# Third stage of an eight-block kernel: two lanes nine rounds ahead of the other two, and the first and last steps of each attention beside other lanes' rounds

## The chip, the cores and the metric

The kernel runs on one core of a Trainium2 chip. The metric is the device time of one execution in microseconds (us). TensorE is called PE, VectorE DVE, ScalarE ACT, GpSimd POOL and SyncE SP.

## The reference, cut to what matters

The input is x, 4096 tokens of 128 channels (16 sequences of 256), and the program is eight blocks in a row, each `x = x + layernorm(block(layernorm(x)))`. The change touches the third of four stages, which holds three of the blocks: `L2_attn`, `L2_ffn` and `L3_attn`.

```python
x = x + ln(L2_attn(ln(x)))   # causal attention, 16 heads of 8 channels
x = x + ln(L2_ffn(ln(x)))    # gelu(x @ w1 + b1) @ w2 + b2, hidden 512
x = x + ln(L3_attn(ln(x)))   # a state space scan, an MLP, causal attention, an MLP

# inside L3_attn
n = rms_norm(xm); vg = n @ in_proj_w          # value and gate, 256 each
value = silu(conv4(value)); Bm, Cm = xm @ B_proj_w, xm @ C_proj_w
y = selective_scan(value, A, Bm, Cm, dt, chunk)
xm = xm + scale * (y * silu(gate) @ out_proj_w)
xm = xm + scale * mlp(rms_norm(xm))           # square(relu(n @ fc)) @ proj
q, k = rope(rms_norm(n @ q_w)), rope(rms_norm(n @ k_w))   # 16 query heads, 4 key heads
y = softmax(causal(q @ k.T)) @ v
xa = xa + scale * (y @ o_w); xa = xa + scale * mlp(rms_norm(xa))
```

## The kernel before

The 4096 tokens are eight groups of 512 tokens (two sequences of 256 each). In stage 3 they go through in two halves of four groups; the four groups of a half are the four *lanes* 0 to 3. A lane has a quarter of the buffer `LN`, a slice of `wAB` for scratch, and two of the eight PSUM banks: lane 0 banks 0 and 1, lane 1 banks 2 and 3, lane 2 banks 4 and 5, lane 3 banks 6 and 7.

Every engine has its own instruction stream, written out in a fixed order by Python generators: a lane's work on an engine is a generator, and each `yield` ends a *round*. `together(gens, lag)` takes one round of each lane in turn, and lane n begins n rounds after lane 0 (`LAG3` is 1). An instruction waits for the semaphores of the engines that it needs, and everything behind it on its engine waits with it.

Stage 3 (`phase3`) is five steps: `l2_in` (normalise, queries, keys, values of the L2 attention), `mid` (output product of that attention, the L2 MLP, the scan, an MLP, and queries, keys, values of the L3 attention), `l3_out` together with `l2_in` of the second half, `mid` again, and `l3_out`. Behind each of the first four steps comes an attention over all lanes (`attend`). In rounds of a lane, `l2_in` has 4, `l3_out` 6 and `mid` 53. Of the 53 rounds of `mid`, rounds 0 to 10 are the L2 output and MLP with five normalisations and the convolution (the *prelude*); rounds 11 to 42 are the scan, two times 16; rounds 43 to 52 (the *tail*) are the MLP (its second product in round 47, PE line L331, with DVE lines L1460 to L1456 and the statistics L237 behind it) and the rotated queries and keys (DVE lines L1554 to L1586 and L1488, in rounds 50 to 52).

An attention works on 32 *quads* (eight for each lane, in the order of the lanes), in 41 steps t from -5 to 35. In step t PE makes the scores of quad t by key in banks 4 to 7 (L388, L395), from which ACT takes the exponentials, and the scores of quad t+5 by query in banks 0 to 3 (L391, L398), from which DVE takes the maxima (L491), both with masks (L378). Each has a first and a second half. So steps -5 to -1 hold scores by query alone, and steps 28 to 35 scores by key, values (L475) and the transposes of results alone (L444, L465). The first exponential of the attention is in step 0.

At the end of stage 2 the four chunks of its result `YA` for each half are scaled, normalised and added to x (`dve_out`, `pool_out`), for all eight groups, before stage 3 begins; POOL gives the reciprocal root of each normalisation (L283).

SP issues nothing in stage 3 but one weight load at its start.

Of the kernel before, what the change touches and what calls it, by code (L numbers as in the profile page):

```python
# [18 lines left out]
LW = 8192  # L19
LAG2, LAG3 = 9, 1  # L20
# [118 lines left out]
def together(gens, lag=0, start=None):  # L139

    live, rnd = dict(enumerate(gens)), 0
    while live:
        for n in sorted(live):
            if rnd >= (start[n] if start else lag * n):
                try:
                    next(live[n])
                except StopIteration:
                    del live[n]
        rnd += 1
# [10 lines left out]
def build(nc, tables, wa, wb, wc, wd, wm, wi, ve, co, step, xin, out):  # L160
    ctx = ExitStack()
    with ctx:
# [197 lines left out]
        PT = [LN[:, LW * i + 6656:LW * i + 8192].rearrange("p (j c) -> p j c", j=4) for i in range(4)]  # L360
        OS = LN[:, 6144:6400].rearrange("p (t c) -> p t c", t=2)
        ON = [LN[:, LW * i + 6144:LW * i + 6400].rearrange("p (t c) -> p t c", t=2) for i in (1, 2)]
# [59 lines left out]
        def pe_attend(pe, banks, k, quads, nb, nw):  # L422
            n = len(quads)
            for t in range(-nb - 1, n + 4):
# [41 lines left out]
                if ins is not None:  # L466
                    ins.then_inc(*P4.inc((k, t, "second")))

        def pe_values(pe, quads, window):
            po = spare(6)  # L470
            for s in window:
                for kt, qt in ((0, 0), (0, 1), (1, 1)):
                    for j in range(4):
                        p = 128 * (kt + qt)
                        ins = pe.e.matmul(po[32 * j:32 * j + 32, qt, :], quads[s].v(kt, j), PT[s % 4][:, j, p:p + 128],  # L475
                                          start=s == window[0] and kt == 0, stop=s == window[-1] and kt == qt)
            return ins

        def dve_attend(dve, k, quads, nb, nw):
# [4 lines left out]
            for x in ON:  # L484
                ins = dve.e.memset(x, 0.0)
            ins.then_inc(*D4.inc())
# [6 lines left out]
            for t in range(-nb - 1, n + 4):  # L493
# [36 lines left out]
                D4.mark((k, t, "second"))  # L530

        def act_attend(act, k, quads, nb, nw):
            n = len(quads)
            for t in range(n + 4):
                w, on = window_at(t, nw, quads), done_at(t - 3, nb, nw, quads)
                if t < n:
                    act.wait_ge(P4, (k, t, "first"))
                    act.e.activation(PT[t % 4][:, 0:2, :], pair(4), ACT.Exp).then_inc(*A4.inc())  # L538
# [7 lines left out]
                if t < n:  # L546
                    act.wait_ge(P4, (k, t, "second"))
                    act.e.activation(PT[t % 4][:, 2:4, :], pair(6), ACT.Exp).then_inc(*A4.inc())  # L548
# [3 lines left out]
                A4.mark((k, t, "second"))  # L552

# [1161 lines left out]
        phi = wAB[:, 0:2048]  # L1715
        MR = MISC[:, 4:36].rearrange("p (m b) -> p m b", m=2)
# [266 lines left out]
        def dve_ya(dve, c, other, q, p):  # L1983
            k, m, gp = ("smoe", q), p // 2, p % 2
            al = views2(c, m)["al"]
            for n in range(2):
# [51 lines left out]
        def dve_out(dve, c, g):  # L2038
            dve.wait_ge(DD[LANES], "rls")
            YG = YA.rearrange("p b m e -> p (b m) e")[:, 4 * g:4 * g + 4, :]  # L2040
# [6 lines left out]
        def pool_out(pool, c, g):  # L2047
            yield from pool_norm(pool, c, (g, "so"))

# [278 lines left out]
        def phase3(eng, ls, l2_in, mid, l3_out, attend):  # L2328

            def stage(eng, c, item):  # L2330
                half, make = item
                yield from make(eng, c, 4 * half + c.n)

            for step, ka in (([(0, l2_in)], ("l2", 0)), ([(0, mid)], ("l3", 0)), ([(0, l3_out), (1, l2_in)], ("l2", 1)),
                             ([(1, mid)], ("l3", 1)), ([(1, l3_out)], None)):
                together([chain(stage, eng, c, step) for c in ls], LAG3)
                if ka is not None and attend is not None:
                    attend(ka, quads23(ls, ka), 4, 2)

        def pe_program(e):  # L2340
# [8 lines left out]
            def attend(ka, quads, nb, nw):  # L2349
                pe_attend(pe, banks, ka, quads, nb, nw)  # L2350
# [27 lines left out]
        def act_program(e):  # L2378
# [5 lines left out]
            def attend(ka, quads, nb, nw):  # L2384
                act_attend(act, ka, quads, nb, nw)
# [21 lines left out]
        def dve_program(e):  # L2407
# [9 lines left out]
            def attend(ka, quads, nb, nw):  # L2417
                dve_attend(dve, ka, quads, nb, nw)
# [13 lines left out]
            run_lanes(dve_out, dve, 1)  # L2432
# [13 lines left out]
        def pool_program(e):  # L2446
# [10 lines left out]
            run_lanes(pool_out, pool, 1)  # L2457
            ended(GD, "p2")
            sync_all(pool, "p2")
            phase3(pool, lanes(), pool_l2_in, pool_mid, pool_l3_out, None)  # L2460
# [206 lines left out]
```

## Time and profile before

| what | value |
| --- | --- |
| median of 3 runs | 3795.21 us (3792.87 to 3801.27) |
| the profiled execution | 3797.36 us |
| its span in the profile | 3795.6 us |
| busy share of the span | PE 78%, DVE 63%, ACT 48%, POOL 14% |
| granted PE clock, mean | 0.868 of full |
| DMA, mean | 7 GB/s |

Busy time is the time in which an engine ran instructions; the rest of the span it waited. The granted clock has two levels, 0.5 (1.2 GHz) and 1.0 (2.4 GHz), and a stretch shows the mean of both. Stage 3 lies between 2031.5 and 3476.7 us of the span. In the trace's windows and timelines the start of a row is in us from the span's start.

### The profile page before, as it was taken

To read this page: it belongs to the slowest core of one execution; us is meant where nothing else is said; L and a number is where in the kernel's file an instruction comes from. 1 tells how busy PE (TensorE), PEld (TensorE's weight loads), DVE (VectorE), ACT (ScalarE), POOL (GpSimd) and SP (SyncE) were. 2 spreads that over 40 slices of the span, in tenths; PEclk is the share of its full clock that TensorE was granted. 3 is DMA by queue.
4 is the path that set the end of the run, shared out by engine and by line. 5 is a ranking of instruction groups with operands and counts; after the bars stand their busy time and mean duration, and the time that the engine had idled before them with its cause. 6 is when DMAs were issued, how large, how long until landed. Compare 5 with 4: busy or idle time off the path is not lost.

```text
span 3795.6 us, 76097 instructions
## 1 busy us (share of the span) xinstructions
PE 2975.8 (78%) x31950; PEld 2354.3 (62%) x31950; DVE 2390.8 (63%) x6446; ACT 1816.6 (48%) x3876; POOL 516.4 (14%) x643
## 2 busy tenths in 40 slices
PE   6788887778888758778884887967778798686885
PEld 3466665456666547667774765856666486574564
DVE  4655555565554578888897666467565845755337
ACT  3556555555555467777773443324434332343222
POOL 1110001120100132222222011120010202002000
PEclk7889988888998879898997988987989899697887
DMA  2000000000000010000000000000000000001000
GB/s 86 1 1 1 1 1 1 1 1 1 1 1 1 1 51 6 7 9 6 7 1 12 2 2 1 2 1 2 2 1 3 1 2 1 1 3 45 1 1 23
DMA packets 13542, 27.99 MB, mean 7 GB/s; under 512 B 784, under 2 KB 9232, under 8 KB 12688
## 3 DMA queue, kind: packets, MB, share of 16 engines
q1 hardware_dynamic: 13200, 23.12, 1.8%
q8 instruction: 252, 4.13, 0.5%
q14 instruction: 90, 0.74, 0.1%
HBM read 21.02 MB, written 2.10 MB: 6 GB/s over the span
## 4 chain that ended last, share of the span: by engine, by line
PE 50%; DVE 36%; ACT 10%; issue 3%; POOL 1%; DMA 0%; SPq 0%; DVEq 0%; POOLq 0%; ACTq 0%
PE ps L331 6%; DVE LN L1944 5%; PE ps L322 4%; PE ps L1822 3%; PE ps L1303 3%; DVE RS L237 3%; PE ps L388 3%; PE ps L296 3%; PE ps L475 3%; DVE M L491 2%; DVE LN L1957 2%; ACT LN L268 2%; PE ps L1314 2%; DVE LN L258 2%; PE ps L1766 1%
## 5 line engine op out<-in xcount | busy, mean ns | idle before, releaser
L304 ACT COPY LN<-ps 128x512 f32<-128x512 f32 (+4 forms) x592 | 303.3, 546 | 629.4 <-PE ps L296 172.2
L283 POOL TENSOR_TENSOR RS<-RS,MISC 128x4 f32<-128x4 f32 x216 | 219.2, 1015 | 2177.2 <-DVE RS L249 1642.6
L296 PE MATMUL ps<-cons,LN 128*128 128x128 f32 x672 | 143.2, 356 | 349.7 <-DVE LN L256 124.8
L296 PEld LDWEIGHTS ps<-cons,LN 128*128 128x128 f32 x672 | 97.8, 178 | 403.7 <-DVE LN L256 143.9
L491 DVE TENSOR_REDUCE M<-ps 128x6 f32<-128x768 f32 x256 | 242.0, 955 | 140.1 <-PE ps L475 95.7
L1944 DVE TENSOR_TENSOR LN<-LN 128x1024 f32<-128x1024 f32 (+2 forms) x192 | 220.3, 1147 | 27.8 <-ACT LN L304 16.9
L388 PE MATMUL ps<-LN 32*128 32x256 f32 x1024 | 187.4, 440 | 53.3 <-DVE LN L527 32.1
L632 DVE TENSOR_REDUCE M<-ps 128x12 f32<-128x1536 f32 x64 | 112.4, 1756 | 175.2 <-PE ps L378 175.2
L322 PE MATMUL ps<-LN,wAB 128*128 128x512 f32 x384 | 207.1, 672 | 14.3 <-ACT LN L341 8.5
L1822 PE MATMUL ps<-LN,wAB 128*128 128x128 f32 x1024 | 150.9, 310 | 74.3 <-ACT LN L304 73.8
L391 PE MATMUL ps<-LN 32*128 32x256 f32 x1024 | 202.9, 475 | 0.8 <-DVE M L491 0.8
L331 PE MATMUL ps<-wAB,LN 128*128 128x128 f32 x1536 | 197.9, 291 | 4.8 <-DVE LN L1469 4.0
L331 PEld LDWEIGHTS ps<-wAB,LN 128*128 128x128 f32 x1536 | 193.0, 207 | 13.1 <-DVE LN L1469 6.3
L1868 ACT ACTIVATE LN<-LN,RS 128x128 f32<-128x128 f32 x512 | 198.7, 400 | 1.6 <-DVE RS L1969 0.6
L2026 POOL TENSOR_TENSOR LN<-LN,M 128x2048 f32<-128x2048 f32 x32 | 146.3, 4571 | 357.2 <-DVE M L1976 357.2
L1822 PEld LDWEIGHTS ps<-LN,wAB 128*128 128x128 f32 x1024 | 143.6, 224 | 78.2 <-ACT LN L304 77.3
L548 ACT ACTIVATE LN<-ps 128x768 f32<-128x768 f32 x128 | 103.7, 810 | 172.0 <-PE ps L475 135.3
L1995 DVE SCALAR_TENSOR_TENSOR LN<-LN,RS,ps 128x128 f32<-128x128 f32 x480 | 127.7, 340 | 48.3 <-PE ps L1822 48.3
L538 ACT ACTIVATE LN<-ps 128x768 f32<-128x768 f32 x128 | 103.8, 811 | 108.6 <-PE ps L378 88.5
L237 DVE BATCH_NORM_STATS2 RS<-LN 128x6 f32<-128x128 f32 x608 | 132.5, 281 | 30.2 <-ACT LN L304 26.0
L1766 PE MATMUL ps<-wAB,LN 128*128 128x128 f32 x1024 | 126.6, 282 | 24.3 <-ACT LN L304 22.9
L388 PEld LDWEIGHTS ps<-LN 32*128 32x128 f32 x1024 | 83.0, 191 | 90.3 <-issue 40.1
(345 smaller groups left out, 7563.3 us busy)
## 6 DMA issues: line engine op xcount, KB each, us to landing
wAB<-wb SPq DMA_DIRECT2D x16, 256.0 KB, 2.7
LN<-wd SPq DMA_DIRECT2D x8, 512.0 KB, 6.9
wAB<-wa SPq DMA_DIRECT2D x1, 3840.0 KB, 16.1
wCs<-wc SPq DMA_DIRECT2D x1, 2336.0 KB, 10.7
XA<-xin SPq DMA_DIRECT2D x8, 256.0 KB, 7.6
y<-XA SPq DMA_DIRECT2D x8, 256.0 KB, 2.3
wAB<-wb SPq DMA_DIRECT2D x1, 1024.0 KB, 5.0
wAB<-wm SPq DMA_DIRECT2D x1, 1024.0 KB, 4.8
```

Source lines behind the costliest of these rows:

```text
L237: dve.e.bn_stats(r[:, 6 * i:6 * i + 6], src[:, i, :]).then_inc(*c.D.inc((k, "stats", i)))
L283: pool.e.tensor_tensor(c.r[:, 40:44], c.r[:, 36:40], mhalf, ALU.pow).then_inc(*c.G.inc((k, "rstd")))
L296: ins = pe.e.transpose(ps[:, n * 128:(n + 1) * 128], src[:, n, :], ident)
L304: act.e.copy(dst, ps).then_inc(*c.A.inc(named(k, done)))
L322: pe.e.matmul(ps[:, :], w1[:, j * 128:(j + 1) * 128], xT, start=True, stop=True).then_inc(*c.P.inc((k, "up", j)))
L331: ins = pe.e.matmul(ps[:, t * 128:(t + 1) * 128], h3[:, j, t * 128:(t + 1) * 128], w2[:, j, :], start=j == 0, stop=j == nh - 1)
L388: pe.e.matmul(psum[n][:, 0:256], qt.ka[rows[j], o:o + 128], qt.qa[rows[j], o:o + 256], start=True, stop=False)
L391: pe.e.matmul(psum[n][:, 128:384], qs.qa[rows[j], o + 128:o + 256], qs.ka[rows[j], o:o + 256], start=True, stop=False)
L491: return dve.e.tensor_reduce(cols[:, 2 - 2 * h:4 - 2 * h, :, q.at], src, X_AX, ALU.max, negate=True)
L1822: ins = pe.e.matmul(psum[2 * gp + n][:, i * 128:(i + 1) * 128], eTb[2 * gp + n][:, i * 128:(i + 1) * 128], v["ym"][:, 4 * g + i, :], start ...
L1868: ins = act.e.activation(v["L3"][:, b, :], v["L3"][:, b, :], ACT.Exp, bias=v["nm"][:, b:b + 1], accum_out=v["rs"][:, b:b + 1])
L1944: dve.e.tensor_tensor(dst, src[:, 0:n, :], src[:, n:2 * n, :], op).then_inc(*c.D.inc())
```

## The change

`phase3` now runs lanes 0 and 1 (*front*) and lanes 2 and 3 (*back*) as two pairs, each with a lag of 1 inside. In each step but the first the back pair starts 9 rounds behind the front pair (`SKEW3`; 2 in the first, which is where it stood). The attention's generators yield after each step, on every engine. Its steps -5 to -1 stand behind the rounds of the back pair, once the front pair has ended its rounds; its steps 0 to 27 stand alone, as before; and its last eight steps, 28 to 35, stand ahead of the first eight rounds of the next step of stage 3. The next step of stage 3 still begins only when the steps 0 to 27 have been put down.

The buffers that the attention used in all lanes' parts of `LN` (exponentials `PT`, results `OS` and `ON`) move to parts of lanes 2 and 3 and of `wAB` that nothing else uses then; there are three buffers of exponentials, in two halves each, where there were four. Two memsets of `ON` go. Of the end of stage 2, `dve_out` and `pool_out` are done for four groups there; for the other four they stand in the first attention, on DVE in its steps 5 to 12, half of a group in each step. For that the last accumulation of stage 2 writes to `wAB` (`YF`) in place of `YA`.

```diff
+def abreast(gens, lag):
+    live, rnd = dict(enumerate(gens)), 0
+    while live:
+        for n in sorted(live):
+            if rnd >= lag * n:
...
+        if live:
+            yield True
+        rnd += 1
...
-        PT = [LN[:, LW * i + 6656:LW * i + 8192].rearrange("p (j c) -> p j c", j=4) for i in range(4)]
...
+        HALVES = [LN[:, LW * c + o:LW * c + o + 768] for c in (2, 3) for o in (6144, 6912)]
+        HALVES += [wAB[:, 1024 * c:1024 * c + 768] for c in (0, 1)]
+        PT = [[x.rearrange("p (j c) -> p j c", j=2) for x in HALVES[2 * i:2 * i + 2]] for i in range(3)]
...
-        def dve_attend(dve, k, quads, nb, nw):
+        def dve_attend(dve, k, quads, nb, nw, side):
...
                 D4.mark((k, t, "second"))
+                if t >= 5:
+                    next(side, None)
+                yield
...
+                        dst = YF if q == 15 else YA
...
+        def dve_out_later(dve, ls):
+            for c in ls:
+                yield from dve_out(dve, c, c.n + 4)
+                yield
...
-                together([chain(stage, eng, c, step) for c in ls], LAG3)
-                if ka is not None and attend is not None:
-                    attend(ka, quads23(ls, ka), 4, 2)
+            ending, skew = iter(()), 2
...
+                front = abreast([stage(c, items) for c in ls[:2]], LAG3)
+                back = abreast([stage(c, items) for c in ls[2:]], LAG3)
+                coming = attend(ka, quads23(ls, ka), 4, 2) if ka else iter(())
+                rnd, ramp, more, last = 0, 5, True, True
+                while last:
+                    next(ending, None)
+                    more = more and next(front, False)
+                    if rnd >= skew:
+                        last = next(back, False)
+                    if not more and ramp and last:
+                        next(coming, None)
+                        ramp -= 1
+                    rnd += 1
+                for _ in ending:
+                    pass
+                for _ in range(ramp + 32 - 5 + 1):
+                    next(coming, None)
+                ending, skew = coming, SKEW3
...
-            run_lanes(dve_out, dve, 1)
+            together([dve_out(dve, c, c.n) for c in lanes()], 1)
```

Line numbers in the changed kernel are higher: for PE, L388 and L395 are now L405 and L412, L391 and L398 are L408 and L415, L378 is L395, L475 is L493, L296 is L311, L314 is L329, L322 is L337, L331 is L346, L1303, L1314, L1324, L1330 are L1322, L1333, L1343, L1349.

On PE, where an attention ends and `mid` begins, there stood before the last scores, the last values (L475) and transposes, and then the output products of two lanes (L314), the transposes (L296) and the first MLP products (L322):

```order
L388 MATMUL ps<-LN 128x256 x2
L395 MATMUL ps<-LN 128x128 x2
L378 MATMUL ps<-cons 128x2x32 x8
L465 MATMUL ps<-cons,LN 128x128 x2
L475 MATMUL ps<-LN 32x128 x24
L465 MATMUL ps<-cons,LN 128x128 x2
L444 MATMUL ps<-cons,LN 128x128 x2
L314 MATMUL ps<-wCs,LN 128x128 x8
L296 MATMUL ps<-cons,LN 128x128 x4
```

Now the output products of lanes 0 and 1 (L329) stand between the scores of the steps 28 to 31:

```order
L329 MATMUL ps<-wCs,LN 128x128 x4
L405 MATMUL ps<-LN 128x256 x2
L412 MATMUL ps<-LN 128x128 x2
L395 MATMUL ps<-cons 128x2x32 x8
L405 MATMUL ps<-LN 128x256 x2
L412 MATMUL ps<-LN 128x128 x2
L395 MATMUL ps<-cons 128x2x32 x8
L482 MATMUL ps<-cons,LN 128x128 x2
L329 MATMUL ps<-wCs,LN 128x128 x4
```

What moved there is eight steps of the attention, which now stand ahead of one round of the front pair each.

On PE, at the end of `mid`, there stood before the tail of four lanes, in which every second product of the MLP (L331) has the transposes of the lane ahead of it (L296) in front:

```order
L331 MATMUL ps<-wAB,LN 128x128 x16
L322 MATMUL ps<-LN,wAB 128x512 x4
L1255 MATMUL ps<-wCs,LN 128x192 x4
L296 MATMUL ps<-cons,LN 128x128 x4
L331 MATMUL ps<-wAB,LN 128x128 x16
L322 MATMUL ps<-LN,wAB 128x512 x2
L1255 MATMUL ps<-wCs,LN 128x192 x4
L296 MATMUL ps<-cons,LN 128x128 x4
```

Now the front pair's tail has scan products of the back pair in it (L1333, L1356, L1343, L1349):

```order
L346 MATMUL ps<-wAB,LN 128x128 x16
L337 MATMUL ps<-LN,wAB 128x512 x2
L1343 MATMUL ps<-wAB,LN 32x128 x8
L1349 MATMUL ps<-cons,LN 128x128 x4
L1333 MATMUL ps<-LN 128x128 x8
L311 MATMUL ps<-cons,LN 128x128 x4
L346 MATMUL ps<-wAB,LN 128x128 x16
L1356 MATMUL ps<-LN 128x32 x4
```

and the back pair's tail has the attention's steps -5 to -1 in it, here two halves of one step (L408, L415, L395) ahead of the second MLP product:

```order
L408 MATMUL ps<-LN 128x256 x2
L415 MATMUL ps<-LN 128x128 x2
L395 MATMUL ps<-cons 128x2x32 x8
L408 MATMUL ps<-LN 128x256 x2
L415 MATMUL ps<-LN 128x128 x2
L395 MATMUL ps<-cons 128x2x32 x8
L346 MATMUL ps<-wAB,LN 128x128 x16
L337 MATMUL ps<-LN,wAB 128x512 x2
```

What moved is that a tail of four lanes is now two tails of two lanes, the first beside scans and the second beside the attention's start.

On DVE, in the first attention, two maxima of a step (now L506) and the division of a window (L539, L542) are followed by the work of `dve_out` on a group of the second half (L2064 scaling, L252 to L264 statistics, L273 and L305 the sum into x), which before stood at the end of stage 2:

```order
L539 RECIPROCAL MISC<-ps 128x16
L542 TENSOR_TENSOR LN<-ps,MISC 128x8x8 x2
L2064 TENSOR_SCALAR wAB<-wAB,MISC 128x128 x4
L252 BN_STATS RS<-wAB 128x6 x4
L255 BN_AGGR RS<-RS 128x2 x4
L264 TENSOR_SCALAR RS<-RS 128x4
L506 TENSOR_REDUCE M<-ps 128x2x3 x2
L532 TENSOR_TENSOR M<-M 128x16
L273 TENSOR_SCALAR wAB<-wAB,RS 128x128 x4
L305 TENSOR_TENSOR XA<-XA,wAB 128x512
```

What moved there is half of a group's work behind each of eight steps.

## Rows read from the trace of the kernel before

**Rows 1.** The page's part 1: busy time of each engine, share of the span, instructions.

```profile
PE 2975.8 (78%) x31950; PEld 2354.3 (62%) x31950; DVE 2390.8 (63%) x6446; ACT 1816.6 (48%) x3876; POOL 516.4 (14%) x643
```

**Rows 2.** Windows of stage 3: stretch, length, busy per engine, PEclk, DMA.

```profile
2031.50:2073.60 42.10, 0.07 (x1) 0.02 (x1) 37.54 (x171) 0.00 (x0) 11.14 (x11) 0.56 0.07 25
...
2073.60:2114.00 40.40, 34.06 (x262) 23.85 (x266) 23.28 (x63) 15.52 (x25) 8.89 (x9) 0.71 0.00 1
...
2114.00:2214.80 100.80, 87.38 (x2422) 75.08 (x2423) 64.88 (x114) 50.05 (x76) 0.00 (x0) 0.98 0.01 3
...
2214.80:2602.80 388.00, 307.40 (x2688) 243.14 (x2692) 239.55 (x717) 124.67 (x222) 59.34 (x72) 0.85 0.00 1
...
2702.80:2819.80 117.00, 87.07 (x736) 65.25 (x740) 71.56 (x228) 35.31 (x57) 20.04 (x20) 0.83 0.00 1
...
2919.30:3299.10 379.80, 298.45 (x2688) 237.36 (x2692) 239.48 (x717) 124.71 (x222) 59.37 (x72) 0.87 0.00 1
...
3399.30:3476.70 77.40, 53.29 (x474) 40.46 (x474) 43.86 (x153) 19.78 (x33) 8.05 (x8) 0.89 0.00 1
```

**Rows 3.** Windows inside the first middle, 2214.8 to 2602.8, same columns.

```profile
2214.80:2235.70 20.90, 18.45 (x266) 14.54 (x267) 1.84 (x9) 7.51 (x12) 0.00 (x0) 0.67 0.01 2
2235.70:2282.50 46.80, 34.63 (x187) 24.08 (x185) 40.12 (x191) 18.28 (x28) 15.16 (x15) 0.88 0.00 1
2282.50:2321.00 38.50, 21.46 (x77) 13.72 (x78) 33.63 (x113) 11.98 (x20) 9.26 (x9) 0.77 0.00 1
2321.00:2475.00 154.00, 154.00 (x1652) 127.68 (x1651) 76.40 (x174) 52.65 (x91) 16.53 (x28) 0.98 0.01 2
2475.00:2586.00 111.00, 62.19 (x322) 49.30 (x320) 76.98 (x217) 31.28 (x67) 18.39 (x20) 0.75 0.00 0
2586.00:2602.80 16.80, 16.67 (x196) 13.82 (x196) 10.58 (x15) 2.97 (x5) 0.00 (x0) 0.50 0.01 1
```

**Rows 4.** Timeline of PE, tail of the middle: start, us, line, idle before.

```profile
2495.85 3.74 PE L331 MATMUL ps<-wAB,LN 128*128 128x128 f32 x32
...
2509.87 5.72 PE L331 MATMUL ps<-wAB,LN 128*128 128x128 f32 x32
...
2524.10 1.02 PE L296 MATMUL ps<-cons,LN 128*128 128x128 f32 x4 [3.78 <-DVE LN L256]
...
2524.91 5.05 PE L331 MATMUL ps<-wAB,LN 128*128 128x128 f32 x32
...
2538.92 1.12 PE L296 MATMUL ps<-cons,LN 128*128 128x128 f32 x4 [5.93 <-DVE LN L256]
```

**Rows 5.** Timeline of DVE, the same tail.

```profile
2515.62 0.69 DVE L1460 TENSOR_TENSOR LN<-ps,vecs 128x512 f32<-128x512 f32 x1 [6.79 <-PE ps L331]
...
2520.59 2.48 DVE L1469 SCALAR_TENSOR_TENSOR LN<-ps,LN 128x512 f32<-128x512 f32 x4
...
2522.98 1.06 DVE L256 TENSOR_SCALAR LN<-LN,RS 128x128 f32<-128x128 f32 x4
...
2574.74 0.82 DVE L1554 TENSOR_TENSOR wAB<-LN 128x640 f32<-128x640 f32 x1
...
2576.45 0.20 DVE L1558 TENSOR_SCALAR wAB<-wAB 128x80 f32<-128x80 f32 x1
...
2577.88 0.64 DVE L1561 RECIPROCAL wAB<-wAB 128x80 f32<-128x80 f32 x1
...
2582.20 0.63 DVE L1586 COPY LN<-LN 128x128 f32<-128x128 f32 x4
...
2584.05 1.41 DVE L1488 TENSOR_SCALAR LN<-ps,cons 128x512 f32<-128x512 f32 x2 [1.21 <-PE ps L296]
```

**Rows 6.** Groups of DVE in the first steps of the second attention.

```profile
L491 DVE TENSOR_REDUCE M<-ps 128x6 f32<-128x768 f32 x10 | 9.6, 958 | 4.2 <-PE ps L378 4.2
```

**Rows 7.** Timelines of PE and DVE, lane 0 in the last item.

```profile
3414.73 1.06 PE L314 MATMUL ps<-wCs,LN 128*128 128x128 f32 x8
...
3451.69 0.69 DVE L290 TENSOR_TENSOR XA<-XA,LN 128x512 f32<-128x512 f32 x1
```

More of the change, by code:

```diff
@@ L530, in dve_attend @@
                 D4.mark((k, t, "second"))
+                if t >= 5:
+                    next(side, None)
+                yield
         def act_attend(act, k, quads, nb, nw):
             n = len(quads)
-            for t in range(n + 4):
+            for t in range(-nb - 1, n + 4):
                 w, on = window_at(t, nw, quads), done_at(t - 3, nb, nw, quads)
-                if t < n:
+                if 0 <= t < n:
                     act.wait_ge(P4, (k, t, "first"))
-                    act.e.activation(PT[t % 4][:, 0:2, :], pair(4), ACT.Exp).then_inc(*A4.inc())
+                    act.e.activation(PT[t % 3][0], pair(4), ACT.Exp).then_inc(*A4.inc())
                 if on is not None:
@@ L545, in act_attend @@
                 A4.mark((k, t, "first"))
[L546 removed]
+                if 0 <= t < n:
                     act.wait_ge(P4, (k, t, "second"))
[L548 removed]
+                    act.e.activation(PT[t % 3][1], pair(6), ACT.Exp).then_inc(*A4.inc())
                 if w is not None:
@@ L2328, in phase3, with stage @@
         def phase3(eng, ls, l2_in, mid, l3_out, attend):
[L2330 to L2335, printed above, removed]
-                together([chain(stage, eng, c, step) for c in ls], LAG3)
-                if ka is not None and attend is not None:
-                    attend(ka, quads23(ls, ka), 4, 2)
+            def stage(c, items):
+                for half, make in items:
+                    yield from make(eng, c, 4 * half + c.n)
+            ending, skew = iter(()), 2
+            for items, ka in (([(0, l2_in)], ("l2", 0)), ([(0, mid)], ("l3", 0)), ([(0, l3_out), (1, l2_in)], ("l2", 1)),
+                              ([(1, mid)], ("l3", 1)), ([(1, l3_out)], None)):
+                front = abreast([stage(c, items) for c in ls[:2]], LAG3)
[16 more added lines that the diff above has]
+                ending, skew = coming, SKEW3
         def pe_program(e):
@@ L2456, in pool_program, with attend @@
                 pool_half(pool, chains(), h)
-            run_lanes(pool_out, pool, 1)
+            together([pool_out(pool, c, c.n) for c in lanes()], 1)
             ended(GD, "p2")
             sync_all(pool, "p2")
-            phase3(pool, lanes(), pool_l2_in, pool_mid, pool_l3_out, None)
+            def attend(ka, quads, nb, nw):
+                yield from idle(10)
+                if ka == ("l2", 0):
+                    for c in lanes():
+                        for _ in pool_out(pool, c, c.n + 4):
+                            pass
+                yield from idle(len(quads) + 4 - 5)
+            phase3(pool, lanes(), pool_l2_in, pool_mid, pool_l3_out, attend)
             ended(GD, "p3")
```

28 lines of the change are left out of this document (16 added, 12 removed).

## The prediction

> **What bounds the kernel now.** I read the page first: PE is busy 78% of the span and DVE 63% [rows 1], so neither is full, and a mean over stages says little. Then I cut stage 3 into windows at the first exponential of attention step 0 and of step 28 [rows 2]. The reader is to see three kinds of stretch. Where the attention is alone (steps 0 to 27) 100.8 us hold 87.4 us of PE at clock 0.98: nearly full. The two long stretches between a step 28 and the next step 0 (I call each a *middle*) take 388.0 and 379.8 us. The short ones are 40.4, 117.0 and 77.4 us, and ahead of them lie 42.1 us in which DVE is busy 37.5 and PE not at all.
>
> The windows inside a middle [rows 3] show that its limits change. The scan is PE alone: 154.0 of 154.0 us busy, DVE half idle at 76.4. The prelude and the tail are neither: in the tail's 111.0 us PE is busy 62.2 and DVE 77.0, at clock 0.75. The timelines say why [rows 4, 5]. The transposes of one lane and of the next (2524.10, 2538.92) start 14.8 us apart, and between them the engines take turns: PE's L331 5.1 to 5.7 us, DVE's scaling, mixing and statistics 5.0 (2515.62 to 2520.59), L1469 of two other lanes 2.5, L256 1.1, and PE transposes again. Four lanes one round apart all need the same engine at once. The attention's ends [rows 3] are thin too: 20.9 us for its last eight steps, with 1.8 us of DVE, and 16.8 us for its first five, with 10.6 us of DVE, at clock 0.67 and 0.50.
>
> **The change, part by part.** The sum is made against the profiled execution, 3797.4 us, 2.2 above the median.
>
> *End of stage 2.* Eight groups take 42.1 us and 37.5 us of DVE, 4.7 a group [rows 2]. Four stay, so 19 us go. The other four cost 18.8 us of DVE inside an attention in which DVE has 64.9 busy in 100.8 us. In the eight steps that take them DVE has 8 x (64.9/28 + 2.35) = 37.3 us to do, where a step lasts 3.6 us, 28.8 in all. The cover is thus 8.5 us too short; DVE can lag some microseconds behind PE with banks in hand, so I take 6 (ends 0 and 8.5). In the first step of the stage the lanes stand as before, but about two of the five first attention steps and the memsets are hidden: 4 us. Together -17.
>
> *The middle.* Rounds 0 to 52 of the front pair and rounds 9 to 62 of the back pair; five parts.
> 1. Rounds 0 to 8, front alone with attention steps 28 to 35. Four lanes need 46.8 us until lane 0's second transposes [rows 3]. For two lanes PE and DVE in strict turns would be (34.6 + 40.1)/2 = 37.4, with ACT and POOL between them; I take 42. The eight attention steps hold 18.5 us of PE work and wait only on PE and ACT; most falls into PE's waits, I add 7. **49** (ends 42 and 54).
> 2. Rounds 9 to 20, front in convolution and scan, back in the prelude. DVE: half a prelude (40.1 + 33.6)/2 = 36.9, the front's own convolution rounds 11, twelve rounds of a pair's scan at 76.4/32/2 = 1.2, 14: 62. Three rounds in between, in which the back pair is in its MLP, are PE's and leave DVE idle some 5 us each: **76** (ends 65 and 84).
> 3. Rounds 21 to 42, all in the scan: 22 x 154.0/32 = **106**. Nothing is gained there.
> 4. Rounds 43 to 53, front in the tail, back in the scan. Turns as now: rounds 43 to 46 some 5.1 each, 20.5 (statistics or L256, transposes, ACT, halves of the MLP, 1.2 of scan; my estimate), then L331 3.7 (at full clock) [rows 4], then DVE 5.0, L1469 1.4, scan of two lanes 1.2, L256 0.9, transposes 0.7, L331 3.7: 12.9; then 5.0 + 1.2 + 0.9; then the rope rounds, of which the last statements take 4.9 and 1.4 [rows 5] and the first 1.9 (2574.74 to 2576.65): 1.9 + 1.2, 4.9 + 1.9 + 1.2, 1.4 + 4.9 + 1.2, 1.4. That makes 64; I take **65** (ends 58 and 77). PE's scan lies inside DVE's turns.
> 5. Rounds 54 to 62, back alone with attention steps -5 to -1. The same turns without the scan, 50; each of the five steps adds two maxima of 0.96 us [rows 6] and, where PE's 3.3 us for it (16.7/5 [rows 3]) are not covered, some more: 10; half clock on two products of L331 (5.7 against 3.7) 4. **64** (ends 50 and 75).
>
> Sum 360, against 388.0 and 379.8: **-28 and -20**. All ends together give 321 and 396.
>
> *The stretch of 117.0 us* (`l3_out` and the second `l2_in`, ten rounds). With a skew of nine the pairs follow each other. Half of PE's and DVE's work in turns would be about (87.1 - 18 - 15 + 71.6 - 2 - 10)/2 = 57; two such are 114, and some overlap inside a pair and one round between the pairs make 45 + 55. Attention steps add 6: **106, -11** (ends 90 and 125).
>
> *The last stretch, 77.4 us.* Lane 0 among four takes from 3414.7 to 3452.4, 37.7 us [rows 7]; a pair 34. Two in a row 68, minus the overlap, plus attention steps 5: **72, -5** (ends 65 and 82).
>
> Steps 0 to 27 of each attention keep their instructions and their order on every engine: 0. Three buffers in place of four cost nothing: the buffer that step t writes was read in step t-1 or earlier, which PE has passed.
>
> Sum: -17 - 28 - 20 - 11 - 5 = **-81**. 3797.4 - 81 = 3716, and on the scale of the median 3714.
>
> A weighing of the skill. Trainium skill, Perfetto Trace Analysis, Optimization Strategy, says that where the most contended engine changes from regime to regime, interleaving the regimes can help. The trace agrees that there are such regimes (154.0 us of PE alone beside 77.0 of 111.0 on DVE); by that rule taken to its end a middle would cost its fullest engine, and the forecast stays above that by parts 1, 4 and 5.
>
> **The rivals.**
>
> *A: more is hidden.* If the turns break up, since one pair's waits are the other's work, the parts come to their lower ends: middles near 323 (-65 and -57), the stretch of 117 at 90 (-27), the last at 67 (-10), the first -19: about -178, 3617. For it: PE's 307.4 us of a middle were done at clock 0.85, and would be some 265 at 0.98. Against it: every stream is in fixed order, so the pair in the tail still holds up the pair in the scan.
>
> *B: the pairs alone are slower than I take.* There are eight lone stretches (two in each middle, two in the 117 us, two in the last). If each takes 10 us more, -81 becomes 0: 3795. For it: four lanes gave something to do in each other's waits, and a lone pair has a lane's whole latency. Against it: the attention's ends fill those stretches.
>
> *C: slower, by the PE clock.* Place: the lone stretches. The row of the attention's first steps shows clock 0.50, and the tail 0.75 [rows 3]. If a lone pair's PE work (17 us in part 1, 31 in part 5) runs at 0.50 in place of 0.88 and 0.75, it takes 13 + 16 us more in a middle, 58 in both, 20 in the 117 us and 15 in the last: +93 - 81 = +12, 3807. It decides from about nine tenths of that price. For it: PE's gaps before lane transposes, 3.8 and 5.9 us [rows 4]. Against it: attention steps stand in exactly those gaps. Trainium skill, TensorE: Matmul & The Clock Gate, section on HAM oscillation, warns of this, that PE idling between bursts puts it back to 1.2 GHz; the row with 0.75 agrees that the tail already suffers.
>
> That the change does not do what it says is no rival: the order of the instructions shows it.
>
> **How the numbers follow.** A measurement of this kernel tells apart about 0.2%, 7.6 us. The forecast (between -50 and -130) has 0.60, A (beyond -130) 0.15, B (between -50 and +8) 0.15, C (slower than +8) 0.10. Within B two fifths are same, the rest faster; so faster 0.84, same 0.06, slower 0.10. The forecast's own range is 3665 to 3745; the range for 8 in 10 takes in most of A and of B: 3630 to 3790.
>
> **What the profile of the changed kernel would show.** The windows between step 28 and step 0: near 360, 106 and 72 us, and PE's clock in them above 0.85. The start of stage 3: PE idle 22 us, not 42. In the scan of four lanes PE full, 4.8 us a round. In the front's tail L331 at 3.7 us, and its repeats about 13 us apart. In the first attention steps 5 to 12 longer than 3.6 us, by 6 us in sum. What would make it wrong: waits of DVE for PE in the lone stretches longer than now, or lone parts at clock 0.5; and, the other way, parts 1 and 5 no longer than the DVE work in them.

## The result, and the profile after

The change makes the kernel slower. Its median is 3856.2 us (3852.66 to 3856.81, four runs) beside 3794.04 for the kernel before on the same chip; the ratio is 1.016 (95% interval 1.014 to 1.018). The forecast was 3714.

The page of the changed kernel, part 1, answers to [rows 1]:

```profile
PE 3015.2 (78%) x31950; PEld 2364.1 (61%) x31950; DVE 2390.2 (62%) x6438; ACT 1823.4 (47%) x3880; POOL 516.7 (13%) x643
```

DVE, ACT and POOL do what they did; PE is busy 39 us longer over the same 31950 matmuls, at a mean granted clock of 0.859 in place of 0.868. Windows of stage 3 in the changed kernel answer to [rows 2] (length, busy PE, PEld, DVE, ACT, POOL, clock; the first row begins at the end of stage 2, and answers to the first two rows of before):

```profile
2035.60:2101.90 66.30, 31.61 (x263) 22.07 (x266) 44.99 (x157) 15.65 (x24) 15.93 (x16) 0.69 0.05 17
2101.90:2209.50 107.60, 89.61 (x2422) 77.23 (x2424) 79.44 (x186) 50.06 (x76) 4.03 (x4) 0.95 0.01 3
2209.50:2614.00 404.50, 313.90 (x2698) 242.51 (x2702) 241.32 (x715) 127.58 (x224) 59.59 (x72) 0.84 0.00 1
2713.50:2839.70 126.20, 92.25 (x734) 64.42 (x732) 70.20 (x227) 35.16 (x57) 20.00 (x20) 0.78 0.00 1
2938.90:3347.80 408.90, 318.25 (x2696) 244.77 (x2700) 241.24 (x715) 127.76 (x223) 59.59 (x72) 0.82 0.00 1
3447.70:3535.60 87.90, 60.04 (x474) 43.82 (x474) 44.74 (x153) 19.82 (x33) 8.05 (x8) 0.80 0.00 1
```

Against [rows 2]: the start 82.5 to 66.3 (-16.2), the first attention 100.8 to 107.6 (+6.8), the middles 388.0 to 404.5 (+16.5) and 379.8 to 408.9 (+29.1), the stretch of 117.0 to 126.2 (+9.2), the last 77.4 to 87.9 (+10.5). With 4.1 us in stages 1 and 2 and -0.2 in stage 4, which the change does not touch, and -1.1 in the other attentions, that is the whole +58.7 of the span (3795.6 to 3854.3).

The five parts of the first middle, in the order of the prediction:

```profile
2209.50:2264.50 55.00, 37.89 (x390) 27.51 (x391) 34.16 (x153) 19.84 (x31) 11.95 (x12) 0.85 0.01 1
2264.50:2355.00 90.50, 69.33 (x404) 48.93 (x403) 57.81 (x192) 35.45 (x57) 15.03 (x16) 0.81 0.00 1
2355.00:2462.80 107.80, 105.53 (x1204) 88.59 (x1202) 56.33 (x138) 31.98 (x55) 14.02 (x23) 1.00 0.01 2
2462.80:2538.90 76.10, 52.11 (x368) 41.12 (x368) 46.97 (x129) 22.59 (x45) 11.62 (x14) 0.80 0.00 1
2538.90:2614.00 75.10, 49.03 (x336) 36.36 (x340) 46.07 (x106) 17.72 (x37) 6.97 (x7) 0.66 0.00 1
```

Predicted were 49, 76, 106, 65 and 64. The scan of four lanes is as forecast; each other part is long. In part 2 DVE has 57.8 us of work, below the 62 it was given, and stands still for 32.7 where 14 were expected. In [rows 3] the prelude of four lanes was 40.12 of 46.80 and 33.63 of 38.50 on DVE, 86 and 87%; here no engine but PE in the scan reaches 80%.

What DVE waits for in part 2, by line (us in total, times, longest):

```profile
DVE wAB L1407 <- PE ps L1333: 11.5, 3, 8.7
DVE LN L1418 <- PE ps L1364: 7.1, 2, 6.0
DVE LN L1539 <- PE ps L346: 4.2, 1, 4.2
DVE RS L252 <- ACT LN L319: 3.5, 1, 3.5
DVE LN L1554 <- ACT LN L1650: 3.5, 3, 1.2
```

and PE in the same window:

```profile
PE ps L311 <- DVE LN L273: 10.5, 2, 10.2
PE ps L311 <- DVE LN L271: 7.0, 2, 3.5
PE ps L311 <- DVE LN L1544: 3.6, 2, 3.0
```

L1407 and L1418 are the front pair's scan on DVE, L311 the transposes behind the back pair's normalisations. DVE stands at a scan statement until PE has the scan product, with the back pair's normalisation behind it; PE stands at a transpose until DVE has normalised, with scan products behind it. Each pair holds up the other in both streams. One such exchange, PE first:

```profile
2284.63 1.12 PE L311 MATMUL ps<-cons,LN 128*128 128x128 f32 x4 [10.19 <-DVE LN L273]
...
2295.78 3.60 PE L337 MATMUL ps<-LN,wCs 128*128 128x512 f32 x8
2299.31 1.16 PE L1333 MATMUL ps<-LN 64*128 64x128 f32 x16
```

and DVE:

```profile
2281.23 2.31 DVE L1558 SCALAR_TENSOR_TENSOR LN<-LN,vecs 128x510 f32<-128x510 f32 x3
2283.46 1.11 DVE L273 TENSOR_SCALAR LN<-XA,RS 128x128 f32<-128x128 f32 x4
...
2300.52 1.29 DVE L1407 TENSOR_TENSOR wAB<-ps,wAB 128x512 f32<-128x512 f32 x2 [8.74 <-PE ps L1333]
```

First PE is idle for 10.2 us, while DVE, which is never idle then, does the front pair's convolution (L1558) ahead of the back pair's normalisation (L273). Then DVE is idle for 8.7 us, while PE does the back pair's MLP product (L337) ahead of the front pair's scan product (L1333).

The lone tail, PE's timeline, answers to [rows 4] (L346 is the second product, L311 the transposes):

```profile
2558.66 3.84 PE L346 MATMUL ps<-wAB,LN 128*128 128x128 f32 x32
...
2571.35 1.12 PE L311 MATMUL ps<-cons,LN 128*128 128x128 f32 x4 [5.40 <-DVE LN L271]
2572.26 5.58 PE L346 MATMUL ps<-wAB,LN 128*128 128x128 f32 x32
...
2586.36 1.12 PE L311 MATMUL ps<-cons,LN 128*128 128x128 f32 x4 [5.28 <-DVE LN L271]
```

and DVE's, which answers to [rows 5]:

```profile
2549.66 0.96 DVE L506 TENSOR_REDUCE M<-ps 128x6 f32<-128x768 f32 x1 [3.00 <-PE ps L395]
...
2570.43 0.86 DVE L271 TENSOR_SCALAR LN<-LN,RS 128x128 f32<-128x128 f32 x4
2577.88 0.69 DVE L1479 TENSOR_TENSOR LN<-ps,vecs 128x512 f32<-128x512 f32 x1 [6.59 <-PE ps L346]
```

Transposes still come 15.0 us apart (14.8 before), with half the lanes, and 14.3 apart in the front's tail. A pair's tail with nothing at all beside it (experiment 7) has them 15.5 apart (2393.91 and 2409.45). So the distance is the turn of one lane through the engines, and half the lanes do not shorten it.

### The profile page after: what moved, and what is told of

It is laid out like the page before. It is cut to its first block, busy times and chain, and to the rows that moved or that the text cites. A ratio compares the mean times of both kernels' runs of the same rounds, so it can differ in the third digit from the quotient of the medians.

```text
span 3854.3 us, 76097 instructions
## 1 busy us (share of the span) xinstructions
PE 3015.2 (78%) x31950; PEld 2364.1 (61%) x31950; DVE 2390.2 (62%) x6438; ACT 1823.4 (47%) x3880; POOL 516.7 (13%) x643
## 4 chain that ended last, share of the span: by engine, by line
PE 49%; DVE 36%; ACT 10%; issue 3%; POOL 1%; DMA 0%; SPq 0%; DVEq 0%; POOLq 0%; ACTq 0%
PE ps L346 6%; PE ps L337 6%; DVE LN L1964 5%; PE ps L1322 3%; PE ps L1842 3%; DVE RS L252 3%; PE ps L311 3%; DVE M L506 2%; PE ps L493 2%; PE ps L405 2%; DVE LN L1977 2%; ACT LN L283 2%; PE ps L1333 2%; DVE LN L273 2%; ACT LN L319 1%
## 5 line engine op out<-in xcount | busy, mean ns | idle before, releaser
L311 PE MATMUL ps<-cons,LN 128*128 128x128 f32 x672 | 146.6, 361 | 349.0 <-DVE LN L271 115.0
L311 PEld LDWEIGHTS ps<-cons,LN 128*128 128x128 f32 x672 | 99.3, 181 | 401.7 <-DVE LN L271 133.5
L506 DVE TENSOR_REDUCE M<-ps 128x6 f32<-128x768 f32 x256 | 240.6, 954 | 133.3 <-PE ps L493 90.5
L337 PE MATMUL ps<-LN,wAB 128*128 128x512 f32 x384 | 223.7, 717 | 17.1 <-ACT LN L356 8.5
L405 PE MATMUL ps<-LN 32*128 32x256 f32 x1024 | 189.2, 444 | 59.9 <-DVE LN L542 31.4
L346 PE MATMUL ps<-wAB,LN 128*128 128x128 f32 x1536 | 190.0, 284 | 8.5 <-DVE LN L1488 7.7
L408 PE MATMUL ps<-LN 32*128 32x256 f32 x1024 | 192.7, 453 | 2.7 <-DVE M L506 2.5
L346 PEld LDWEIGHTS ps<-wAB,LN 128*128 128x128 f32 x1536 | 184.3, 199 | 17.0 <-DVE LN L1488 9.5
L1842 PEld LDWEIGHTS ps<-LN,wAB 128*128 128x128 f32 x1024 | 143.6, 224 | 78.1 <-ACT LN L319 77.3
L252 DVE BATCH_NORM_STATS2 RS<-LN 128x6 f32<-128x128 f32 x576 | 125.5, 281 | 41.5 <-ACT LN L319 37.6
L337 PEld LDWEIGHTS ps<-LN,wAB 128*128 128x128 f32 x384 | 82.0, 230 | 104.8 <-issue 73.7
L1786 PE MATMUL ps<-wAB,LN 128*128 128x128 f32 x1024 | 126.6, 282 | 24.3 <-ACT LN L319 22.9
L405 PEld LDWEIGHTS ps<-LN 32*128 32x128 f32 x1024 | 83.4, 192 | 97.0 <-issue 44.0
L2016 DVE SCALAR_TENSOR_TENSOR LN<-LN,RS,ps 128x128 f32<-128x128 f32 x448 | 119.2, 339 | 34.1 <-PE ps L1842 34.1
L1786 PEld LDWEIGHTS ps<-wAB,LN 128*128 128x128 f32 x1024 | 122.7, 199 | 24.8 <-ACT LN L319 23.1
## 6 DMA issues: line engine op xcount, KB each, us to landing
wAB<-wa SPq DMA_DIRECT2D x1, 3840.0 KB, 16.8
wCs<-wc SPq DMA_DIRECT2D x1, 2336.0 KB, 10.5
```

The costliest lines, as they stand in the source:

```text
L252: dve.e.bn_stats(r[:, 6 * i:6 * i + 6], src[:, i, :]).then_inc(*c.D.inc((k, "stats", i)))
L311: ins = pe.e.transpose(ps[:, n * 128:(n + 1) * 128], src[:, n, :], ident)
L337: pe.e.matmul(ps[:, :], w1[:, j * 128:(j + 1) * 128], xT, start=True, stop=True).then_inc(*c.P.inc((k, "up", j)))
L346: ins = pe.e.matmul(ps[:, t * 128:(t + 1) * 128], h3[:, j, t * 128:(t + 1) * 128], w2[:, j, :], start=j == 0, stop=j == nh - 1)
L405: pe.e.matmul(psum[n][:, 0:256], qt.ka[rows[j], o:o + 128], qt.qa[rows[j], o:o + 256], start=True, stop=False)
L506: return dve.e.tensor_reduce(cols[:, 2 - 2 * h:4 - 2 * h, :, q.at], src, X_AX, ALU.max, negate=True)
```

## The experiments

Each kernel is the changed one with another loop in `phase3`: the skew, whether the attention's last eight steps stand beside rounds, and whether its first five do, are set for each of the five items. "Alone" means that no step of the attention stands beside a round. The kernel before was timed again with each batch of experiments: 3785.21 us with experiments 1 to 4, 3788.72 with 5 to 8, 3796.64 with 9 to 12. So experiments of different batches are compared by their ratios to it. The loop, here with the settings of experiment 3:

```diff
+            plan = zip((2, 9, 9, 9, 9), (False, False, False, False, False), (False, False, False, False, False), (1, 1, 1, 1, 1))
...
+                if not beside:
+                    for _ in ending:
+                        pass
...
+                    if ramped and not more and ramp and last:
```

**1. Only the end of stage 2 moved** (skew 2, all alone: PE's stream is that of the kernel before).

> Lanes one round apart as before, all attention steps alone; of the change only the second half of dve_out and pool_out in the first attention, the new buffers and the two memsets less per attention are left. Both theories (lone pairs take turns; attention steps stand in the way) say the same here: the changed kernel's trace has 16 us less ahead of the first attention, some 4 of them from the ramp, and 7 us more in it. So 3794 - 12 + 7 - 2 = about 3787; the middles stay at 388 and 380 us.

Measured: 3781.34 beside 3785.21, ratio 0.9993 (0.9984 to 1.0002). The first exponential comes at 2097.7 in place of 2114.0, and the first attention is 7.4 us longer (108.2): +9 of gain in the trace, of which 0.07%, some 3 us, is left in the times, and the interval includes no gain at all. The stretches that this kernel shares with the one before differ by up to 7 us between the two profiles (first middle 381.4 and 388.0, last stretch 84.9 and 77.4), so that is how finely one stretch of one profile can be read.

**2. The lag as before, the first five steps beside the last rounds** (skew 2).

```diff
-            plan = zip((2, 2, 2, 2, 2), (False, False, False, False, False), (False, False, False, False, False), (1, 1, 1, 1, 1))
+            plan = zip((2, 2, 2, 2, 2), (False, False, False, False, False), (True, True, True, True, True), (1, 1, 1, 1, 1))
```

> As the run with dve_out moved alone, and the attention's steps -5 to -1 begin beside the last rounds of lanes 2 and 3, without a skew of nine. Only about three steps find a round (the first stage step: two). Lone pairs take turns: attention steps in waits are nearly free, so 4 x some 6 us less than the run before it, about 3765. Attention steps stand in the way: each holds the lane behind it up by its own length, no gain, 3787 or a little more.

Measured: 3765.85, ratio 0.9958 (0.9945 to 0.9972). This version beats both kernels. Its gain over the first experiment is some 15 us, as expected if attention steps fill waits. Where it lies the profiles do not show: the spans differ by 10.0, the middles are 380.8 and 376.8 and the stretch 120.4, and 7.9 of the 10.0 lie in the last stretch, in which both kernels have the same instructions in the same order (experiment 1, then experiment 2):

```profile
3383.74:3468.60 84.86, 61.20 (x474) 45.55 (x474) 44.21 (x153) 19.82 (x33) 8.06 (x8) 0.82 0.00 1
3381.09:3458.10 77.01, 52.15 (x474) 39.95 (x474) 43.39 (x153) 19.83 (x33) 8.06 (x8) 0.91 0.00 1
```

The same 474 matmuls keep PE busy 61.2 us at clock 0.82 and 52.2 at 0.91. With nothing else different in the stretch, the lower clock goes with 7.9 us more.

**3. The skew of nine alone.**

> The skew of nine rounds, but every attention step alone. Lone pairs take turns: this holds the whole loss and none of the gain, so it is the slowest: 3856 plus what the overlap of attention steps hides, four times 14 to 20 us at the end and 16 at the start, less what it costs, so about 3856 + 70 = 3925. Attention steps stand in the way: the skew itself gains some 20 us a middle, and this comes out below 3790.

Measured: 3879.47, ratio 1.0249 (1.0235 to 1.0263). All of the loss, and more, is the skew's (98 us over experiment 1): middles 417.7 and 415.0, the stretch 137.2.

**4. The skew of nine with the last eight steps beside rounds.**

> The skew of nine with the attention's last eight steps beside the front pair, its first five alone. Lone pairs take turns: 8 to 12 us less for each of four attentions than the skew alone, about 3885, and more than 3856, since the first five steps are not hidden. Attention steps stand in the way: about the time of the skew alone or more.

Measured: 3850.32, ratio 1.0171 (1.0156 to 1.0187). The eight steps give back 29 us, 7 to 10 for each attention. The changed kernel adds the first five steps to this, and its ratio is 1.016 (1.014 to 1.018): by the ratios these give 4 us, and by the intervals nothing or up to some 14.

**5 and 6. The same rounds in reversed order** (lane 3 ahead of lane 2 ahead of lane 1 ahead of lane 0 in each round; the back pair ahead of the front pair), for experiment 2 and for the changed kernel.

```diff
-        for n in sorted(live):
+        for n in sorted(live, reverse=True):
...
-                    more = more and next(front, False)
                     if rnd >= skew:
                         last = next(back, False)
+                    more = more and next(front, False)
```

> As the run with the first five attention steps beside the last rounds at the old lag, but in every round the lanes come in the order 3, 2, 1, 0. If the loss comes from turns that the order forces (a lane's second MLP product stands behind the transposes of the lane ahead, which wait for DVE's work on that lane), then the product of the next lane now stands right behind the product of the lane ahead, and the tails and preludes of four lanes get shorter too: 10 to 30 us a middle, about 3730. If the loss is plain latency of a lane's own chain, the order does nothing: 3766, within 8.

> The changed kernel with the order of lanes in a round reversed (back pair before front pair, lane 1 before lane 0). Forced turns: at least a third of the 61 us lost comes back, below 3835. Plain latency of a lone pair: 3846, within 10.

Measured: 3834.06, ratio 1.0126 (1.0107 to 1.0144) at the lag of before; 3838.53, ratio 1.0136 (1.0119 to 1.0153) at a skew of nine. With a skew of nine this is what a pair's plain latency was expected to give, and its interval overlaps that of the changed kernel. At the lag of before the reversal costs 1.7%, some 64 us, over experiment 2 with the same instructions and the same rounds (middles 404.7 and 405.4), which no expectation had. So the order of statements inside a round is worth as much as the whole change. In the prelude of the reversed kernel (2225 to 2341.4, 116.4 us with 80.0 of DVE) DVE waits

```profile
DVE LN L1539 <- PE ps L346: 20.1, 3, 10.7
```

where experiment 1, not reversed, has in its own (2226 to 2324.5, 98.5 us with 83.3 of DVE)

```profile
DVE LN L1539 <- PE ps L346: 1.9, 2, 1.0
```

**7. Two pairs one behind the other in each middle** (skew 60 there, 2 elsewhere, all alone).

> Both middles with lanes 2 and 3 only after lanes 0 and 1 are through (a skew of 60 rounds), everything else at the old lag, attention steps alone. If what costs is that a lone pair needs its own latency, this shows it whole: prelude 55, scan 77 to 110, tail 70 us for each pair, with the attention's ends some 440 to 510 us a middle, where the skew of nine had 416. If the cost was the pairs in different parts holding each other up, a middle is shorter than with nine, 380 to 400.

Measured: 3911.82 in its one run; middles 445.7 and 446.3, as expected if a lone pair needs its own latency. From the first output product to the next step 0 two pairs in a row take 430.3 us, and four lanes in lockstep (one round apart) 365.9: both are sums of windows below. The windows of the first middle give what a lone pair's parts cost: prelude (first output product to first scan product), scan, tail, first of the front pair, then of the back pair, whose tail holds the attention's steps -5 to -1.

```profile
2221.60:2275.90 54.30, 31.71 (x134) 19.49 (x132) 35.02 (x148) 16.54 (x26) 11.95 (x12) 0.75 0.00 1
2275.90:2365.60 89.70, 80.46 (x850) 63.07 (x850) 42.93 (x100) 26.59 (x46) 9.80 (x17) 1.00 0.00 1
2365.60:2427.60 62.00, 32.90 (x135) 24.02 (x134) 38.19 (x97) 14.65 (x31) 7.63 (x8) 0.64 0.00 0
2427.60:2483.80 56.20, 33.57 (x133) 20.81 (x132) 35.81 (x150) 18.73 (x29) 11.97 (x12) 0.73 0.00 1
2483.80:2573.60 89.80, 80.56 (x850) 63.17 (x850) 42.92 (x100) 26.60 (x46) 9.89 (x17) 1.00 0.01 1
2573.60:2651.90 78.30, 49.17 (x331) 36.92 (x333) 49.59 (x112) 18.76 (x37) 7.55 (x8) 0.63 0.00 1
```

A lone scan round is 89.7/32 = 2.8 us, with PE 90% busy. Now the mixed parts can be read. Experiment 3 does the same middle in the five parts of the prediction:

```profile
2221.50:2270.80 49.30, 27.46 (x126) 17.47 (x125) 32.32 (x144) 12.43 (x19) 11.97 (x12) 0.76 0.00 1
2270.80:2357.00 86.20, 65.00 (x378) 46.04 (x377) 54.08 (x185) 33.11 (x53) 15.05 (x16) 0.80 0.00 1
2357.00:2464.20 107.20, 107.20 (x1189) 89.36 (x1187) 55.70 (x127) 34.33 (x60) 11.86 (x20) 1.00 0.01 2
2464.20:2537.20 73.00, 51.83 (x402) 41.05 (x401) 43.92 (x122) 20.29 (x41) 12.80 (x16) 0.84 0.00 1
2537.20:2620.90 83.70, 52.50 (x337) 39.18 (x339) 55.21 (x131) 20.22 (x39) 8.01 (x8) 0.60 0.00 1
```

The second row, rounds 9 to 20, is 86.2 us for a back prelude (54.3 or 56.2 alone), the front's last two prelude rounds (54.3 - 49.3 = 5.0) and ten of its scan rounds (28.0). One behind the other these are 87.3 or 89.2. In the second middle, by the same marks, they are 86.3 mixed and 87.9 or 91.0 in a row. So here the two pairs, with different work for different engines, overlap by 1 to 5 us: next to nothing, and less than one profile can tell apart.

The other parts overlap somewhat more. The scan of four lanes, 22 rounds, takes 107.2 us where two lone pairs take 44 x 2.8 = 123. The last two rows, 156.7 together, hold a front tail (62.0 alone), ten back scan rounds (28.0) and a back tail (78.3): 168.3 one behind the other, 11.6 more. With 16 us of the scan and 3 of the second row that is the whole difference between the two kernels, 430.3 and 399.4. Experiment 1 does the same middle in three parts, prelude, scan, tail of four lanes:

```profile
2221.40:2324.50 103.10, 73.25 (x342) 50.23 (x342) 85.09 (x323) 41.50 (x68) 24.44 (x24) 0.85 0.00 1
2324.50:2473.30 148.80, 144.33 (x1641) 120.42 (x1640) 74.67 (x195) 44.00 (x75) 21.79 (x35) 0.98 0.01 2
2473.30:2587.30 114.00, 69.58 (x444) 56.47 (x447) 77.27 (x188) 31.91 (x67) 13.22 (x14) 0.71 0.00 1
```

Its ends take 103.1 + 114.0 = 217.1, those of the skew of nine 49.3 + 86.2 + 73.0 + 83.7 = 292.2, 75.1 more; the part in which all four lanes are in the scan shrinks by 148.8 - 107.2 = 41.6. The difference, 33.5, is the loss of the middle.

**8. A skew of four, steps 28 to 31 alone and 32 to 35 beside rounds, the first five beside.**

```diff
+            plan = zip((2, 4, 4, 4, 4), (True, True, True, True, True), (True, True, True, True, True), (1, 1, 1, 1, 1))
...
+                for _ in range(4):
+                    next(ending, None)
```

> A skew of four in the last four stage steps: attention steps 28 to 31 alone, the light steps 32 to 35 beside rounds 0 to 3, back pair from round 4, first five steps beside the last rounds. Lone rounds cost some 5 us each over the old lag of two; so two more lone rounds a stage step cost 4 x 8, the light steps give 4 x 5 back: about 3766 + 12 = 3778, between the old lag and nine, far from 3856. If the skew's loss does not grow with its rounds, 3840 or more.

Measured: 3829.38, ratio 1.0113 (1.0091 to 1.0136). Two more rounds of skew than experiment 2 cost some 59 us, by the ratios. The loss is not in proportion to the skew.

**9 to 12. Skews of three, four and six, and an even lag of two** (lanes at rounds 0, 2, 4, 6), all alone. The edit from experiment 3 to the even lag:

```diff
-            plan = zip((2, 9, 9, 9, 9), (False, False, False, False, False), (False, False, False, False, False), (1, 1, 1, 1, 1))
+            plan = zip((2, 4, 4, 4, 4), (False, False, False, False, False), (False, False, False, False, False), (1, 2, 2, 2, 2))
```

> The back pair three rounds behind the front in the middle and short stages (before: two), every attention alone. In the profile the middles (381.4 and 379.8 us with a skew of two and the same attentions, 417.7 and 415.0 with nine) tell. Drawn-out rounds, 5.1 us for each extra round of skew, since 36 us came with seven: middles 386 and 385, total +13 us over a skew of two. Broken step, where a pair that is not one round behind its neighbour costs most of the 36 at once: middles of 397 or more, total +30 or more.

> The same with a skew of four. Drawn-out rounds: middles 392 and 390. Broken step: 400 or more, and little more than with three. It also tells how much of the 22 to 24 us that a skew of four cost in each middle of the kernel with the light steps beside was the light steps' doing: none, if the middles here are above 402.

> The same with a skew of six. Drawn-out rounds: middles 402 and 400. Broken step: 405 to 412, on a flat line between three and nine.

> Each lane two rounds behind the one before it (lanes at rounds 0, 2, 4 and 6 in place of 0, 1, 2 and 3), every attention alone: three more rounds for each item, and no gap larger than another. Drawn-out rounds: middles 397 and 395, near the line between skew four and six. Broken step, if it is the uneven gap that costs: under 395; if any gap other than one costs: 405 or more.

| lanes at rounds | middles | stretch of ten rounds | time | ratio |
| --- | --- | --- | --- | --- |
| 0, 1, 2, 3 (experiment 1) | 381.4, 379.8 | 117.1 | 3781.34 | 0.9993 |
| 0, 1, 3, 4 | 392.5, 395.4 | 121.9 | 3817.46 | 1.0055 (1.0029 to 1.0082) |
| 0, 1, 4, 5 | 405.6, 404.0 | 127.1 | 3843.24 | 1.0129 (1.0065 to 1.0194) |
| 0, 1, 6, 7 | 397.2, 397.9 | 135.6 | 3852.23 | 1.0153 (1.0123 to 1.0183) |
| 0, 1, 9, 10 (experiment 3) | 417.7, 415.0 | 137.2 | 3879.47 | 1.0249 |
| 0, 2, 4, 6 | 409.0, 406.8 | 135.8 | 3866.62 | 1.0191 (1.0148 to 1.0234) |
| 0, 1, 60, 61 in middles (experiment 7) | 445.7, 446.3 | 117.3 | 3911.82 | |

Neither of the two theories in these expectations held throughout. Drawn-out rounds at 5.1 us each is too little at three and four (11 to 16 us for one round, 24 for two); one step at once is too much at three, and fits four and the even lag of two (405 or more expected, 409.0 and 406.8 measured). The middles of a skew of six come out 6 to 8 us shorter than those of four, which is about what one profile can tell apart, and the profile of four is of the slower of its two executions (3852.62 and 3833.85); in the times, six is not faster. What holds throughout: in this order of lanes any spacing but one round costs, an even lag of two too. The light steps of experiment 8 neither cost nor give anything in its middles (404.8 and 401.6), which are those of a skew of four alone; its stretch of ten rounds is 115.3 beside 127.1.

The prelude of four lanes at a skew of four, in a window from 20 us after step 28 (5 us after the first output product) to lane 3's first scan product:

```profile
2232.00:2354.60 122.60, 82.89 (x388) 56.27 (x388) 84.81 (x317) 40.37 (x66) 23.18 (x23) 0.79 0.00 1
```

and the same window of experiment 1:

```profile
2226.00:2324.50 98.50, 71.38 (x325) 48.55 (x326) 83.28 (x313) 39.96 (x65) 23.43 (x23) 0.85 0.00 0
```

DVE's work is the same to 1.5 us; its idle time goes from 15.2 to 37.8. Of that the waits with a name are

```profile
DVE LN L1554 <- ACT LN L1650: 17.3, 4, 7.1
DVE LN L1539 <- PE ps L346: 7.5, 2, 5.9
DVE RS L252 <- ACT LN L319: 5.7, 1, 5.7
```

against 3.5, 1.9 and 0.2 us for the same three pairs of lines in experiment 1. (The longer window also holds 63 more matmuls, of scan rounds that have begun.) Four lanes one round apart, in this order, keep DVE 85% busy in the prelude; another spacing leaves it, as these waits show, without work while a lane's is with PE or ACT. The reversed order of experiment 5 leaves it idle too, 36.4 of 116.4 us, at a spacing of one round.

## Why the prediction was wrong

**The end of stage 2.** -23 and +6 were taken, -16.2 and +6.8 measured. The price in the attention was right. At the start DVE's part ahead of the first PE row fell from 42.1 to 26.4, 3 us less than forecast, and the 4 us taken for hidden first steps and memsets are not there (40.4 us before, 39.9 now).

**Part 3, the scan of four lanes:** 106 taken, 107.8 measured, right; steps 0 to 27 of the other attentions: right.

**Parts 1, 2, 4 and 5 of a middle: here the prediction failed.** They were priced at 49 + 76 + 65 + 64 = 254; measured are 55.0 + 90.5 + 76.1 + 75.1 = 296.7. The failed sentence is "The prelude and the tail are neither", with what was drawn from it: that four lanes one round apart get in each other's way, and that another pair's waits can be filled. [Rows 3] spoke against it: 40.12 of 46.80 and 33.63 of 38.50 us of DVE is an engine 86% full, and only the tail was loose (76.98 of 111.0, with the last rounds at 81%, by 46.26 of 57.0 from 2545.8 on). Parts 2 and 4 were built as sums of DVE's work with PE's scan "inside DVE's turns". Beside the serial kernel this hardly happens: the mixed rounds of part 2 cost nearly what both pairs' rounds cost one behind the other (86.2 and 87.3 to 89.2), and parts 4 and 5 together save 11.6 of 168.3. Part 2's DVE work was taken a little high (62, measured 57.8); the term that was mis-sized is its idle time, taken at 14 and measured at 32.7. Part 2's failure is thus one of overlap, and that of parts 1 and 5 one of a lone pair's own latency. Part 1 gave the pair 42 and the attention steps 7; without the steps the pair takes 49.3 (experiment 3), and with them 55.0. Part 5 gave the pair 50; experiment 3 has 83.7 with the five steps behind it, 67 without their 16.8 [rows 3]. The transposes of two lanes were priced 12.9 us apart in the front's tail and came 14.3 apart.

The skew of nine without any attention step beside rounds (experiment 3) puts the loss on the skew, and the eight steps beside rounds (experiment 4) are a gain, as forecast: 29 us of it.

**The stretch of 117.0 and the last stretch.** 106 and 72 were forecast, 126.2 and 87.9 measured. "Some overlap inside a pair and one round between the pairs" gave 45 + 55; in experiment 3, with nothing beside, the stretch is 137.2, and in lockstep 117.1.

**The rivals.** A is refuted: the fixed order did hold up each pair by the other, as the sentence against A said. B (eight lone stretches 10 us slower each) names the right kind of loss in half of the places: parts 1 and 5 are 6 and 11 us over the forecast, the stretch of 117.0 us is 20 over it and the last 16, with two lone stretches each, as B priced them; but the mixed parts, which B left alone, are 14.5 and 11 over. A time this much slower was given to C alone (0.10). C asked for clock 0.50 in lone pairs; they have 0.85 and 0.66, so its condition is not met.

The clock is even so a part of the loss, and the runs do not separate it. The two last stretches under experiment 2 show what a lower clock goes with where the instructions are the same: 8 us in 77. In this kernel's middles PE is busy 6.5 and 19.8 us longer than before over nearly the same matmuls. Beside the first middle of experiment 1 PE is busy 19.6 us longer in that of experiment 3, which is 36.3 longer (clock 0.81 and 0.87), and 9.6 longer at a skew of four, which is 24.2 longer. If all of PE's added time lay where it is waited for, which the runs do not show, the clock would be about half of the loss at nine and two fifths at four. The rest is waiting.

The prediction weighed what the Trainium skill, Perfetto Trace Analysis, Optimization Strategy, says, that interleaving regimes in which different engines are the most contended may improve performance. Little of it is borne out here: scan rounds, 90% PE, beside prelude rounds, 65% DVE in a lone pair, gave 1 to 3 us in 88, and beside a tail 12 in 168. The exchange at 2284.63 shows why for this kernel: its engines work through streams in fixed order, and a handoff of either pair stops both.

**Left open:** which meetings of rounds cost most at skews of three to six; why a reversed order costs so much only at the lag of before, beyond DVE's longer wait for L346; how much of the loss is the clock; whether DVE's work bounds the prelude of four lanes, since no experiment gave DVE less of it; and where the 15 us of experiment 2 lie.

## What to carry to other kernels

When groups share in-order streams, do not count on two different phases overlapping because they use different engines: here a handoff of one group stopped the other too. Measure the lone cost of each phase first (a serial version does it in one run), and compare the mixed rounds with the sum. Look at each engine's share window by window: DVE had 63% of the span and 86% of the prelude, and there a regrouping is to be priced by what keeps this engine fed, not by its work alone. And where a change has an arrangement part and an overlap part, try the overlap alone: here it was worth 0.4%, and the arrangement cost 2.5%.

## What the runs showed of the hardware that was not expected

In the changed kernel's lone tail four products of L337 took 3.78 us at 2540.73 and 1.88 us at 2562.33, and 32 of L346 3.84 and 5.58 us within 14 us: the granted clock was 0.50 in the first of these four (2540.7 to 2544.5, PE busy for 1.1 of the 4.2 us before it) and 1.00 in the second (2562.3 to 2564.2, behind 15 us of matmuls without a gap). It goes between its two levels inside one tail, as in [rows 4]. The lone pair's scan ran at clock 1.00 in 89.7 us with PE 90% busy: half the lanes did not lower the clock where PE was the full engine. The lone pair's prelude and tail ran at 0.75 and 0.64, where those of four lanes in experiment 1 had 0.85 and 0.71. And the same stretch with the same instructions ran at 0.82 in one profile and 0.91 in another, 8 us apart.
